# Gate weights prepared by GpSimd in the first stage, and tile rows cleared one piece a strip

## The reference, cut to what matters

```
h = window_attention_8x8(x)                # 8 heads, rotary positions
h = h + local_attention_7x7(layernorm(h))
h = h + expert_ffn(layernorm(h))           # the expert is chosen per 256 tokens
h = h + decayed_retention(layernorm(h))    # linear attention, alpha = 0.99
h = h + binary_ffn(layernorm(h))
```

```
gate = (sigmoid(einsum('hbi,ei->hbe', xh, proj_w) + proj_b) > 0.5)
w = einsum('hbe,heio->hbio', gate, weight)      # 8 gated 64x64 matrices
y = einsum('hbi,hbio->hbo', sign(xh), sign(w)) * scale
```

## Time and profile before

| what | value |
|---|---|
| median of 3 runs | 1696.08 us (1695.56 to 1696.74) |
| the profiled execution's own time | 1696.52 us |
| its span, first to last instruction | 1694.7 us |
| TensorE busy | 1537.1 us, 91% |
| VectorE busy | 1211.7 us, 71% |
| ScalarE busy | 1048.5 us, 62% |
| GpSimd busy | 614.7 us, 36% |

### The profile page before, as it was taken

The page is one execution under the profiler, slowest core; times in us unless marked ns, Lnnn a source line. Parts: engine busy times, 40 slices in busy tenths (PEclk is TensorE's granted clock), DMA queues, the critical chain, the costliest instruction groups (busy, mean ns, idle before and its releaser), DMA issues.

```text
span 1694.7 us, 85491 instructions
## 1 busy us (share of the span) xinstructions
PE 1537.1 (91%) x30842; PEld 1101.6 (65%) x30842; DVE 1211.7 (71%) x3605; ACT 1048.5 (62%) x2053; POOL 614.7 (36%) x925
## 2 busy tenths in 40 slices
PE   7999999889999999999974799999999999999997
PEld 5777777767777777777763565665665565655662
DVE  2566665557878888887754887877877877877872
ACT  3556556434444444444421488888888888888887
POOL 3332232266666666666623222222222222222210
PEclk9999999989999999999986899999999999999996
DMA  4101010044444444444420345445445445445443
GB/s 129 62 26 31 25 31 25 14 117 119 120 121 124 125 123 121 122 121 121 124 72 23 62 81 91 85 79 91 85 79 92 85 79 92 85 79 92 85 81 62
DMA packets 128724, 143.31 MB, mean 85 GB/s; under 512 B 36626, under 2 KB 84114, under 8 KB 128402
## 3 DMA queue, kind: packets, MB, share of 16 engines
q1 hardware_dynamic: 120338, 116.17, 33.5%
q10 hardware_dynamic: 8320, 26.22, 5.7%
HBM read 66.55 MB, written 16.99 MB: 49 GB/s over the span
## 4 chain that ended last, share of the span: by engine, by line
PE 64%; issue 9%; ACT 9%; DMA 6%; DVE 5%; POOL 3%; SPq 2%; ACTq 1%; DVEq 1%; POOLq 0%
PE ps_D L924 9%; DMA k_d<-kpad 4%; ACT prob L1237 4%; PE ps_AV L943 4%; PE ps_D L702 3%; PE ps_D L831 3%; PE ps_J L1001 3%; PE ps_OT L850 3%; PE ps_J L1035 2%; PE ps_OT L1011 2%; PE ps_J L1066 2%; PE ps_J L986 2%; PE ps_AV L858 2%; PE ps_OT L1077 2%; PE ps_AV L712 2%
## 5 line engine op out<-in xcount | busy, mean ns | idle before, releaser
L1237 ACT ACTIVATE prob<-ps_D 128x1024 bf16<-128x1024 f32 x448 | 459.5, 1029 | 112.5 <-PE ps_D L924 111.8
L1207 ACT ACTIVATE prob<-ps_D 100x512 f32<-100x512 f32 x256 | 138.8, 594 | 167.2 <-PE ps_D L831 167.2
L567 POOL TENSOR_TENSOR tile_a<-q_st,q_mask 128x512 f32<-128x512 f32 x128 | 135.1, 1055 | 117.7 <-PE ps_D L831 106.0
L831 PE MATMUL ps_D<-tile_a,key_patch 64*100 64x128 f32 x2048 | 177.2, 291 | 0.0
L827 PE MATMUL ps_D<-mT,key_rows 64*100 64x128 bf16 x1024 | 124.7, 228 | 25.0 <-ACT prob L1207 25.0
L1399 DVE TENSOR_REDUCE m_sb<-ps_D 128x4 f32<-128x400 f32 x256 | 134.5, 566 | 11.3 <-PE ps_D L808 11.0
L831 PEld LDWEIGHTS ps_D<-tile_a,key_patch 64*100 64x100 f32 x2048 | 141.2, 168 | 0.0
L541 POOL TENSOR_TENSOR rstd_bin<-veps_bin,minus_half 128x2 f32<-128x2 f32 x64 | 44.1, 689 | 264.7 <-DVE veps_bin L1298 264.7
L541 POOL TENSOR_TENSOR rstd_ret<-veps_ret,minus_half 128x2 f32<-128x2 f32 x64 | 47.3, 739 | 241.8 <-DVE veps_ret L1298 241.8
L924 PE MATMUL ps_D<-tile_b,w_parts 64*64 64x256 bf16 x2048 | 104.4, 287 | 14.3 <-ACT prob L1237 11.8
L924 PE MATMUL ps_D<-tile_a,w_parts 64*64 64x256 bf16 x2048 | 101.9, 282 | 15.7 <-ACT prob L1237 12.1
(11 more groups left out here) (185 smaller groups left out, 3957.7 us busy)
## 6 DMA issues: line engine op xcount, KB each, us to landing
tile_a<-xg SPq DMA_DIRECT2D x192, 128.0 KB, 4.2
tile_b<-xg SPq DMA_DIRECT2D x192, 128.0 KB, 4.3
key_st<-k_d SPq DMA_DIRECT2D x128, 162.0 KB, 3.0
tile_b<-v_d ACTq DMA_DIRECT2D x128, 120.0 KB
tile_b<-v_d ACTq DMA_DIRECT2D x64, 160.0 KB
w_exp<-experts SPq DMA_DIRECT2D x64, 129.0 KB, 2.2
xT<-in_x SPq DMA_DIRECT2D x32, 256.0 KB, 2.6
k_d<-kpad SPq DMA_DIRECT2D x64, 64.0 KB, 2.9
```

Source lines behind the costliest of these rows:

```text
L567: gp.tensor_tensor(q_block[:, par, :].rearrange("c (p h q) -> c p h q", h=NH, q=NQ)[:, own, :, :], q_st[:, par, :].rearrange("c (p a q) -> ...
L831: mm = pe.matmul(s_loc[x][0:NKL, u * P:(u + 1) * P], key_patch[rows_of(x), par, at * NKL:(at + 1) * NKL], q_block[rows_of(x), par, at * P: ...
L1207: act.activation(prob1[0:NKL, 2 * g + x, :], s_loc[x][0:NKL, :], ACT.Exp).then_inc(T2["exp_done"], 1)
L1237: act.activation(sgn[:, k % 4, :], unit(k, par)[:, :], ACT.Sign).then_inc(BN["sign"], 1)
```

## The change

Four things are changed.

- The w_bin load is issued in the 8x8 stage, behind the last of the constant loads (experts) and ahead of the loop over x_in.
- GpSimd makes the gate weights, one piece (`gate_weights(n)`, n from 0 to 12) behind each `tok_turned` of iterations 8 to 20. The steps differ a little: each of the three parts is multiplied in place by its own column of the part mask, the three are added up, and the sum is multiplied by two lane masks into w_parts. The tiles used on the way are others (xg, hidT, q_sb, key_st), and part_mask has 5 columns for 6. VectorE keeps only the copy of w_qk3.
- The four clearings go into steps 1 to 4 of the last stage, each behind that step's `inv_std("ret", ...)` on GpSimd.
- SyncE no longer waits for the clearings before its first step, but before the first `spread_in`, in step 4. TensorE's wait for them ahead of strip 0's first w_parts product stays.

```diff
@@ SyncE
                     x_in(n // 8 + 1, (n // 8 + 1) % 2)
+            sp.dma_start(w_bin, a["w_bin"]).then_inc(s_gate_w, 16)
             with sp.Fori(2, NT // 2) as j:
...
                 if g is not None:
+                    if isinstance(g, int) and g == 0:
+                        sp.wait_ge(s_clear, 4)
                     spread_in(g, par)
 
             sp.wait_ge(T2["h_done"], times(NS))
-            sp.dma_start(w_bin, a["w_bin"]).then_inc(s_gate_w, 16)
-            sp.wait_ge(s_clear, 4)
             staggered(sp, strips)
@@ GpSimd, 8x8 stage
-            with gp.Fori(4, NT // 2) as j:
+            def gate_weights(n):
...
+                if n == 2:
+                    gp.wait_ge(s_gate_w, 16)
+                    gp.tensor_copy(w_high, w_bin).then_inc(s_placed, 1)
+                if n == 3:
+                    gp.wait_ge(s_placed, 5)
+                    gp.tensor_tensor(w_rest, w_bin, w_high, ALU.subtract).then_inc(s_placed, 1)
...
+                if 6 <= n < 9:
+                    gp.wait_ge(s_placed, n + 2)
+                    part = (w_high, w_mid, w_low)[n - 6]
+                    gp.tensor_tensor(part, part, part_mask[:, n - 6:n - 5].broadcast_to((P, 1024)), ALU.mult).then_inc(s_placed, 1)
...
+                if 11 <= n < 13:
+                    gp.wait_ge(s_placed, 13)
+                    gp.tensor_tensor(w_parts[:, :, :, n - 11, :], w_high.rearrange("p (n h o) -> p n h o", n=16, h=2),
+                                     part_mask[:, n - 8:n - 7].rearrange("p (a b c) -> p a b c", a=1, b=1).broadcast_to((P, 16, 2, 32)), ALU.mult).then_inc(s_placed, 1)
+
+            for n in range(14):
+                tok_turned(8 + n, n % 2)
+                gate_weights(n)
+            with gp.Fori(11, NT // 2) as j:
@@ GpSimd, last stage
             gp.wait_ge(T2["h_done"], times(NS))
-            for n, (tile, at) in enumerate(((tile_a, 32), (tile_a, 96), (tile_b, 32), (tile_b, 96))):
-                if n:
-                    gp.wait_ge(s_clear, n)
+            def clear_rows(n):
+                tile, at = ((tile_a, 32), (tile_a, 96), (tile_b, 32), (tile_b, 96))[n]
                 gp.memset(tile[at:at + 32, :, :], 0.0).then_inc(s_clear, 1)
-            gp.wait_ge(s_clear, 4)
+                gp.wait_ge(s_clear, n + 1)
...
                 if f is not None:
                     inv_std("ret", RT, f)
+                if isinstance(j, int) and 1 <= j < 5:
+                    gp.wait_ge(FF["biased"], times(j + 1))
+                    gp.wait_ge(RT["rstd"], times(j))
+                    clear_rows(j - 1)
@@ VectorE, last stage
-            def gate_weights(j):
-                if j == 0:
...
-                    dve.tensor_copy(w_high, w_bin).then_inc(s_placed, 1)
-                    dve.wait_ge(s_placed, 4)
-                    dve.tensor_tensor(w_rest, w_bin, w_high, ALU.subtract).then_inc(s_placed, 1)
-                if j == 1:
...
-                if j in (2, 3, 4):
-                    for lane in range(2):
...
-                if isinstance(j, int):
-                    gate_weights(j)
+                if isinstance(j, int) and j == 0:
+                    dve.wait_ge(s_qk, 1)
+                    dve.tensor_copy(w_qk3[:, :], bank["AV"][:, C:C + P]).then_inc(s_qk, 1)
```

More of the change, by code:

```diff
@@ L118, in shape_tables @@
     half, part, lane = np.arange(P) // 64, np.arange(P) % 64 // 16, np.arange(P) % 16 // NG
-    t["part_mask"] = ((part[:, None, None] == np.arange(3)[None, :, None]) & (lane[:, None, None] == np.arange(2)[None, None, :])).astype(np.float32).reshape(P, 6)
+    t["part_mask"] = np.concatenate([part[:, None] == np.arange(3), lane[:, None] == np.arange(2)], 1).astype(np.float32)
     spread = np.zeros((P, 4, P), np.float32)
@@ L165, in build @@
         w_gate, b_gate = sb("w_gate", [P, P]), sb("b_gate", [P, 1])
-        w_parts, part_mask = sb("w_parts", [P, 16, 2, 2, 32], BF16), sb("part_mask", [P, 6])
+        w_parts, part_mask = sb("w_parts", [P, 16, 2, 2, 32], BF16), sb("part_mask", [P, 5])
         spread_f, spread = sb("spread_f", [P, 4 * P]), sb("spread", [P, 4 * P], BF16)
@@ L202, in build @@
         x_parts = [tile_a[:, :, :].rearrange("p a n -> p (a n)").bitcast(BF16), tile_b[:, :, :].rearrange("p a n -> p (a n)").bitcast(BF16)]
-        w_bin, w_rest = key_patch[:, :, :].rearrange("p a n -> p (a n)")[:, 0:1024], key_rows[:, :, :].rearrange("p a n -> p (a n)")[:, 0:1024]
-        w_high, w_mid, w_low = rot[:, 0, :].bitcast(BF16), rot[:, 1, :].bitcast(BF16), q_sb[:, :, :].rearrange("p a n -> p (a n)").bitcast(BF16)
+        w_bin, w_rest = key_patch[:, :, :].rearrange("p a n -> p (a n)")[:, 0:1024], key_st[:, :, :].rearrange("p a n -> p (a n)")[:, 0:1024]
+        w_high, w_mid, w_low = xg[:, :], hidT[:, :, :].rearrange("p a n -> p (a n)")[:, 0:512].bitcast(BF16), q_sb[:, :, :].rearrange("p a n -> p (a n)").bitcast(BF16)
         ysum, ys, yo = sb("ysum", [P, 512], BF16), sb("ys", [P, 2, C]), sb("yo", [P, 2, C])
@@ L527, in _ @@
                                  shared[:, l, :].rearrange("p (a n) -> p a n", a=1).broadcast_to((P, NEXP + 1, HID + 1)), ALU.add).then_inc(s_prep, 1)
-            with gp.Fori(4, NT // 2) as j:
+            def gate_weights(n):
+                if n == 0:
+                    gp.tensor_copy(spread[:, :], spread_f[:, :]).then_inc(s_placed, 1)
+                if n == 1:
+                    gp.tensor_copy(lane_sum[:, 0, :], lane_sum_f[:, :]).then_inc(s_placed, 1)
+                    gp.tensor_scalar(lane_sum[:, 1, :], lane_sum_f[:, :], 1.0 / TINY, None, ALU.mult).then_inc(s_placed, 1)
+                    gp.tensor_copy(half_sum[:, :], half_sum_f[:, :]).then_inc(s_placed, 1)
+                if n == 2:
[4 more added lines that the diff above has]
+                    gp.tensor_tensor(w_rest, w_bin, w_high, ALU.subtract).then_inc(s_placed, 1)
+                if n == 4:
+                    gp.wait_ge(s_placed, 6)
+                    gp.tensor_copy(w_mid, w_rest).then_inc(s_placed, 1)
+                if n == 5:
+                    gp.wait_ge(s_placed, 7)
+                    gp.tensor_tensor(w_low, w_rest, w_mid, ALU.subtract).then_inc(s_placed, 1)
+                if 6 <= n < 9:
+                    gp.wait_ge(s_placed, n + 2)
+                    part = (w_high, w_mid, w_low)[n - 6]
+                    gp.tensor_tensor(part, part, part_mask[:, n - 6:n - 5].broadcast_to((P, 1024)), ALU.mult).then_inc(s_placed, 1)
+                if 9 <= n < 11:
+                    gp.wait_ge(s_placed, n + 2)
+                    gp.tensor_tensor(w_high, w_high, (w_mid, w_low)[n - 9], ALU.add).then_inc(s_placed, 1)
+                if 11 <= n < 13:
[6 more added lines that the diff above has]
+            with gp.Fori(11, NT // 2) as j:
                 tok_turned(j * 2, 0)
```

25 lines of the change are left out of this document (3 added, 22 removed).

## The result

The changed kernel took 1702.24 us by the median of 8 runs (1699.04 to 1706.03) against 1696.26 for the kernel before on the same chip (8 runs, 1692.38 to 1699.50): ratio 1.0036, 95% interval 1.0022 to 1.0050. It is 6.0 us slower, where 5.2 us faster was forecast, and it lies outside the predicted range. The profiled execution took 1703.5, its span 1701.7, which is 7.0 more than the 1694.7 before.

The account below looks back on a forecast made before the run. TensorE paces the last stage's steady part, so time was to be had in its filling. The terms -7.4 - 4.3 + 6.2 + 0.3 = -5.2 gave a median of 1690.9 us, 8 in 10 between 1684.5 and 1693.6.

Parts of the forecast that it names:

- The x lines: Strip 0's transfers behind the fourth clearing: landed by 958 to 959, TensorE wants them at 960.04; cost nothing.
- B: Filling of the last stage, from the last local h to the first w_parts product; forecast -5.5 us.
- The clock term: TensorE's granted clock in the filling: moved strips shift which product meets which level; 0, with 2 us either way.
- The w_bin load: At the start, ahead of iteration 4's xT: may lengthen TensorE's stall near 48 us; 0.3 taken, bounds 0 and 1.3.
- rival (b): Start: w_bin load lengthens the 48 us stall by 1.3 and what follows by about as much; 1693.9, chance 0.13.
- The clearings leave the head: Head of the last stage's filling: first expert product starts at 902.8 for 910.24; minus 7.4 us.
- The clearings come back: Strips 1 to 4, behind rstd_ret: each clearing holds the second xn_r on VectorE, 1.55 a strip; plus 6.2 us.
- rival (a): Strips 1 to 4: clearings hold the kd instructions, not xn_r, 1688.9, or neither, 1684.7; chance 0.27.
- The gate work leaves VectorE: Strips 1 to 4 of the filling: without gate work between veps_ret and xn_r, xn_r starts earlier; minus 4.3 us.
- GpSimd's pieces: Iterations 8 to 20 of the 8x8 stage: added gate pieces fit GpSimd's idle time, up to 6.4 each; cost nothing.
- rival (c): 8x8 stage: GpSimd's pieces exceed their cover, eleven at 7.3 us costing 10; 1700.7, chance 0.05.
- The prediction's own bound: Forecast wrong if the filling, h_done to strip 0's first w_parts product, shrinks by less than 3 or over 8 us.

Follow-up runs that it names:

- e3: Changed kernel with SyncE waiting for two clearings before strip 0's x lines and four before strip 1's; 1691.61 us, ratio 0.9977 to the kernel before.
- e5: Changed kernel, x wait and early load kept, with twelve unused identity products added on TensorE in step 5; 1694.24 us, ratio 0.9989 to the kernel before.
- e2: Changed kernel with the w_bin load moved behind the fetches of iterations 4 and 5; 1696.95 us, ratio 1.0001 to the kernel before.
- e9: Kernel before with only the clearings moved behind rstd_ret of steps 1 to 4, and SyncE's wait for them moved; 1699.75 us, ratio 1.0026.
- e1: Kernel before with one extra early w_bin load behind experts, the old load kept; 1699.33 us, ratio 1.0019.
- e6: e4 with each clearing moved behind the b_o addition, one step earlier, instead of behind rstd_ret; 1686.20 us, ratio 0.9942 to the kernel before.
- e11: The kernel of e6 run once more, beside e10; 1685.42 us, ratio 0.9948 to the kernel before.
- e10: The kernel of e4 run once more, beside e11; 1688.38 us, ratio 0.9956 to the kernel before.
- e4: Changed kernel with the edits of e2 and e3 together; 1687.72 us, ratio 0.9949 to the kernel before.

## Why the prediction was wrong, step by step

**The failed step is "The x lines".** It gave them "nothing, with 1 to 2 us in hand", because TensorE wants them at 960.04. The transfers themselves were reckoned right: landed 7 to 8 us behind the fourth clearing's end by the forecast, 8.1 in the trace (948.58 to 956.7). But TensorE's products are not the first that wait for them. VectorE's xg of step 5 waits for the same semaphore, `BN["x_in..."]`, because it overwrites the transfers' source, and in the frame in which the forecast had the lines land at 958 to 959 it started at 956.81. So the forecast's own numbers, set against the right instruction, give a wait of 1.2 to 2.2; it measured 2.4, in B. The wait stands in the code, and in no row of before, since it cost nothing there. No rival had it.

**The clock term, 0 with 2 either way,** was sized for shifts of phase, not for an idle time of TensorE at the very end of the filling. Measured: +6.2, 5.7 of it in the strips behind that one wait (C is 731.7 and 731.6 in e3 and e5). The wait and its clock make 8.6 of the 12.2 us between forecast and profile. That the clock term came out at 6.2 is this execution's size: the same wait cost 4.6 in C in e2 and 3.2 in e9.

**The w_bin load** was a term mis-sized, less surely: 0.3 with 1.3 as its end, measured 2.5 in its own stage of the changed kernel and 0.8 to 1.1 in that of e1, e3 and e5; by the median e1 is 3.5 slower, between 0.5 and 5.9. That is what rival (b) said, to which I gave 0.13 and 3 us above the forecast: the stall grows, and in the changed kernel's execution what follows it grows as well. The reason given there, that the stall is a fetch behind the same traffic, isn't shown: the stall names no releaser in any trace. What is shown is that it grows with the load in front, from 0.82 to between 1.6 and 1.9.

**The clearings leave the head:** right, -7.4 forecast and 7.4 measured. **The clearings come back:** right in mechanism and nearly in size, 4 x 1.55 forecast, 4 x 1.44 measured on the pairs, and 5.1 of B comes back where they are moved off the xn_r (e6, e11). So rival (a) is excluded: no kd is stretched. One premise was wrong without harm to the sum: the forecast let the first xn_r pass, and it is held as well; since both end with the clearing, the pair takes the same. **The gate work leaves VectorE:** not measured by itself. B of e9 against B of e2, which differ in this and in the w_bin load's place, gives 3.2 for the forecast's 4.3; as B moves by 2.1 unedited (e1), that neither confirms the 4.3 nor corrects it. **GpSimd's pieces:** right, nothing; rival (c) is excluded with 2.13 us for the longest piece against a cover of 6.4.

B alone was forecast at -5.5. With the x wait of 2.4 taken off, the trace's -3.0 is -5.4, which is in part luck, with B moving by 2 us unedited. The prediction's own bound, that it is wrong if the filling shrinks by less than 3, was just met, and still the kernel is slower: the bound looked at one piece of three.

Both faults are in the placing and not in the work moved. With the load behind two more fetches and the x lines' wait split in two, the same change is 0.44 to 0.51% faster than before (e10, e4), and with the clearings off the xn_r 0.52 to 0.58% (e11, e6), the best of these kernels by the median.

## What to carry to other kernels

When a transfer is made later, list all that wait for its semaphore, the engine that overwrites its source among them, and take the slack from the earliest; waits that cost nothing before are in the code, not in the trace. A wait just where TensorE's dense part begins costs its own length and then the clock: 2.6 us idle cost 3.2 to 6.2 more here, and filler products in the wait gave back the second part. A load added to a full queue at the start can lengthen a stall that already stands behind that queue; look whether the clock falls there too, and move the load behind it.

## What the runs showed of the hardware that I had not expected

- The granted clock fell to 1.2 GHz behind 2.6 us of idle time that came right after it had risen, and it was at 1.2 GHz until nearly 976, in rows where TensorE is busy 3.8 to 4.0 of 4 us. Behind much the same idle time it was up again after some 14 us in e2 and some 10 in e9.
- Behind a stall of 0.82 us near 48 us the clock fell in five executions and stayed up in one (e10); behind the three of 0.54 to 0.56 it stayed up.
- A clearing on GpSimd holds both xn_r of a pair to its own end (1.94 and 1.74 us for 0.31 each), the first of them too, which started 0.09 ahead of it.
- Pieces of a kernel that no edit touches differ between kernels: A is 893.3 to 897.8 in the nine without the early load, and e1's filling, with the code of before, is 2.1 longer than before's.
- A GpSimd mask or addition of 1024 elements in bf16 takes 1.89 or 2.12 us and an f32 subtraction 2.13, all about 2 ns an element, while a cast from f32 to bf16 takes 1.04.
